# A decoder layer on one core: pieces of the first batch's scan moved ahead of the query rotations on VectorE, and the normalization in front of the feed-forward part shared out between GpSimd, ScalarE and VectorE

## The chip, the cores and the metric

The kernel runs on one core of one Trainium2 chip. The metric is the device time of one execution in microseconds (us). The program is written by hand for each engine: TensorE (PE in the profile), VectorE (DVE), ScalarE (ACT), GpSimd (POOL) and SyncE (SP) each have their own instruction stream, and they meet only at semaphores.

## The reference, cut to what matters

Four sequences ("batches") of 512 tokens with 512 features go through one decoder layer. All of it is float32.

```
x = x + attention(layernorm(x))            # 16 query heads, 2 key/value heads of 32, rotary, causal
x = x + scan(ctx, z = layernorm(x))        # selective state-space scan, 512 channels, 16 states
x = x + ffn(layernorm(x))                  # 1408 wide, 2 of 8 low-rank experts per token

layernorm(x) = (x - mean(x)) / sqrt(var(x) + 1e-5)

# scan, for each of the 16 states n (h runs over the 512 tokens):
h   = h * exp(dt * A[n]) + (dt * u) * B[n]
y  += h * C[n]                             # then y + D*u, times silu(z)
```

## The kernel before, in words

A 512x512 activation lies in SBUF as four **row tiles** of 128 tokens each, or, transposed, as four tiles of 128 features. The batches are processed one after the other, but the stages of two neighbours overlap: while the feed-forward part of batch t runs on TensorE, VectorE already works on the scan of batch t+1. The first batch has no feed-forward part in front of it, so its scan starts when its own projections start.

**The scan.** One state costs VectorE three instructions over 128x2048 elements, which the code calls pieces: `mul` (L1147, `du * B`), `run` (L1152, the scan itself) and `out` (L1157, times `C`). In front of the first `mul` stands one piece `du`. ScalarE makes `exp(dt * A[n])` for each state (L585, four instructions of 128x511, `make_decay`) and fetches the rows of B and C by DMA (L575, `load_bc`). GpSimd adds each finished state to `y_sb` by an accumulating DMA (L500, `add_states`). `state` and `decay` have two buffers, so `mul` of state n waits until state n-2 has been added, and `make_decay` of state n waits until `run` of state n-2 is done.

**The order of the work.** `plan` takes a list that says how many pieces each slot gets and lays 49 pieces (1 + 3x16) out in order. The slots are first those of the feed-forward part (none for the first batch), then 11 slots f = 0 to 10 (the down projection of the batch before; in the first batch only the projections of the attention stand there), then 32 slots s = 0 to 31, one for each pair of heads and row tile of the attention. `plan` also puts the DMA of B and C and the decay of each state into slots. For the first batch the list `PLAN_FIRST` is: one piece in each of f = 0 to 6, then `SPREAD`, which spreads the rest evenly over f = 7 to 10 and s = 4 to 30.

In slot f VectorE runs the slot's pieces and then `rotate(b, f)`: three 128x512 instructions (L1171, L1174, L1178) that turn the projection made two slots ago (f = 2 to 5 the queries, f = 6 the keys, followed by the copy of the values, L1183). TensorE makes the projections (L809) and their rotated halves (L816) in two PSUM banks; ScalarE moves each projection out of PSUM (L614, `project`). From f = 7 on the first four steps of the attention begin, the rest run in slots s. In each attention step TensorE computes scores (L848, L851), VectorE takes the row maxima (L1188) and the reciprocal of the step before (L1193), ScalarE the exponentials (L626) and moves the transposed probabilities (L638), TensorE weighs the values (L880), and VectorE divides (L1201).

**The normalization in front of the feed-forward part** (kind "ffn", `second_sum`). For each row tile VectorE adds the gated scan to x (L1263), takes mean and variance (`deviation`: L1078, L1081, L1082, L1084), and, one tile later, scales the tile before (`scaled`, L1088). GpSimd computes `(var + eps) ** -0.5` in between (`rstd`, L490). TensorE transposes each scaled tile (L967, `ffn_head`) and ScalarE moves it to `xt` (L591, `transposed_ffn`). For all but the last batch TensorE puts a projection of the next batch, two matmuls of 128x512 (L764), between the transposes of tiles 1 and 2, and ScalarE copies such projections for the convolution (L535, L536) before `transposed_ffn` and after it. When all four tiles are moved, TensorE computes the router (L971) and the wide tiles of the feed-forward part (L932).

```
for i in range(NT + 1):                                   # second_sum, before
    if i < NT:
        ...
        tt(xb[:, i, :], ps_a[:, i, :], xa[:, i, :], ALU.add).then_inc(x2_summed, 1)
        ...
        deviation("ffn", t, xb, i)
    if i >= 1:
        scaled("ffn", t, xb, xn, i - 1)
```

## Time and profile before

| | |
|---|---|
| median of 3 runs | 1403.96 us (1403.82 to 1404.07) |
| the profiled execution: its own time, its span | 1403.27 us, 1401.4 us |
| TensorE matmul busy | 1283.1 us, 92% of the span |
| VectorE busy | 1025.1 us, 73% |
| ScalarE busy | 677.3 us, 48% |
| GpSimd busy | 89.0 us, 6% |
| mean granted TensorE clock | 0.935 of full speed |
| chain that ended last, by engine | PE 61%, DVE 23%, ACT 7% |

The shares are means over stages with different limits. The 40 slices of the page give VectorE 9 or 8 tenths and TensorE 6 to 8 tenths in the slices 3 to 6 (about 70 to 245 us), with a granted clock of half speed, and from slice 8 on TensorE 8 or 9 tenths at nearly full clock. A time in a timeline is counted from the span's start. An instruction's duration reaches a little into the next one's start (pipelining), so the distance between two starts is what it takes of the engine.

### The profile page before, as it was taken

Reading aid. Unit: us, or ns where it says so; the run is one execution under the profiler, and the core shown is the slowest. Engines: PE = TensorE matmul, PEld = TensorE weight load, DVE = VectorE, ACT = ScalarE, POOL = GpSimd, SP = SyncE. Lnnn points to the kernel's source line nnn. Section 1 sums busy time; section 2 is a strip of 40 time slices with the busy share of each in tenths; the row PEclk is TensorE's granted clock in tenths of the full one; section 3 lists DMA queues with packets and bytes.
Section 4 is the critical chain, followed back from the end, with each engine's and each line's share of the span. In section 5 each row is a group of like instructions: output and inputs, shape, how many; then the busy total and the mean of one; then the engine's idle time right before and its main releaser. Section 6 shows DMA issues by size and latency. Waiting matters only on the chain.

```text
span 1401.4 us, 15839 instructions
## 1 busy us (share of the span) xinstructions
PE 1283.1 (92%) x5680; PEld 625.0 (45%) x5680; DVE 1025.1 (73%) x1238; ACT 677.3 (48%) x1465; POOL 89.0 (6%) x116
## 2 busy tenths in 40 slices
PE   5867778899999999899999999899999999799999
PEld 2334444444444465444444465444444465444443
DVE  6799997788899765888899765788899764511110
ACT  5356553465552485465552485465552385211110
POOL 0000001010000000000000000000000000100000
PEclk8855558999999999999999999999999999899999
DMA  6277663147777510147777510147777510011121
GB/s 239 57 187 147 155 138 61 46 114 192 191 188 169 158 33 1 46 115 191 191 189 168 158 32 1 46 114 191 182 187 176 145 25 9 16 38 56 57 64 52
DMA packets 53196, 158.50 MB, mean 113 GB/s; under 512 B 4992, under 2 KB 10880, under 8 KB 44672
## 3 DMA queue, kind: packets, MB, share of 16 engines
q0 software_dynamic: 9216, 67.11, 23.9%
q1 hardware_dynamic: 25520, 54.01, 11.7%
q10 hardware_dynamic: 18384, 36.37, 8.8%
q8 instruction: 46, 0.75, 0.2%
q14 instruction: 30, 0.25, 0.1%
HBM read 85.91 MB, written 4.46 MB: 64 GB/s over the span
## 4 chain that ended last, share of the span: by engine, by line
PE 61%; DVE 23%; ACT 7%; issue 4%; DMA 3%; ACTq 1%; DVEq 0%; POOL 0%
PE ps_a L932 20%; PE ps_a L946 10%; DVE state L1152 9%; PE ps_a L1023 6%; PE ps_b L957 5%; DVE state L1147 4%; PE ps_w L912 4%; PE ps_a L848 3%; ACT r L626 3%; DVE state L1157 3%; PE ps_b L865 2%; DVE neg_max L1188 2%; PE ps_a L986 2%; DMA y_sb<-state 2%; PE ps_w L880 2%
## 5 line engine op out<-in xcount | busy, mean ns | idle before, releaser
L932 PE MATMUL ps_a<-xt,w_sb 128*128 128x512 f32 x704 | 312.1, 595 | 0.0
L1152 DVE TENSOR_TENSOR_SCAN state<-decay,state 128x2048 f32<-128x2048 f32 (+1 forms) x82 | 284.4, 3477 | 2.5 <-ACT decay L585 0.6
L932 PEld LDWEIGHTS ps_a<-xt,w_sb 128*128 128x128 f32 x704 | 133.3, 191 | 170.2 <-issue 170.2
L694 ACT ACTIVATE r<-ps_a 128x512 f32<-128x512 f32 x132 | 78.5, 597 | 255.1 <-PE ps_a L946 139.0
L1334 DVE TENSOR_TENSOR r<-r,ps_a 128x512 f32<-128x512 f32 x132 | 90.0, 683 | 136.2 <-ACT r L694 136.2
L946 PE MATMUL ps_a<-r,wb_sb 128*128 128x512 f32 x352 | 165.6, 593 | 6.5 <-DVE r L1334 6.5
L585 ACT ACTIVATE decay<-dt_sb,decay_rate 128x511 f32<-128x511 f32 x256 | 163.0, 710 | 4.2 <-DVE state L1152 3.8
L626 ACT ACTIVATE r<-ps_a,neg_max 128x384 f32<-128x384 f32 (+3 forms) x224 | 121.8, 562 | 62.8 <-DVE neg_max L1188 57.2
L1157 DVE TENSOR_TENSOR state<-state,bc_sb 128x2048 f32<-128x2048 f32 (+1 forms) x73 | 147.6, 2022 | 1.5
L1147 DVE TENSOR_TENSOR state<-du_sb,bc_sb 128x2048 f32<-128x2048 f32 x64 | 146.1, 2283 | 2.9 <-DMA y_sb<-state 2.0
L865 PE MATMUL ps_b<-cst,r 128*128 128x128 f32 x640 | 109.5, 309 | 26.4 <-ACT r L626 8.8
L848 PE MATMUL ps_a<-r 32*128 32x384 f32 (+3 forms) x448 | 110.7, 575 | 22.4 <-ACT r L626 22.4
L500 POOL DMA_DIRECT2D y_sb<-state x64 | 55.9, 873 | 813.8 <-DVE state L1157 742.9
L946 PEld LDWEIGHTS ps_a<-r,wb_sb 128*128 128x128 f32 x352 | 66.2, 190 | 90.6 <-issue 87.3
L1188 DVE TENSOR_REDUCE neg_max<-ps_a 128x2 f32<-128x768 f32 (+3 forms) x112 | 95.7, 855 | 10.5 <-PE ps_a L851 8.8
L1023 PE MATMUL ps_a<-w_sb,r 128*128 128x512 f32 x224 | 101.2, 594 | 0.0
L865 PEld LDWEIGHTS ps_b<-cst,r 128*128 128x128 f32 x640 | 80.9, 159 | 38.5 <-issue 24.6
L957 PE MATMUL ps_b<-r,ad_sb 128*128 128x512 f32 x176 | 83.1, 594 | 4.9 <-DVE r L1334 4.9
L638 ACT ACTIVATE xt<-ps_b 128x256 f32<-128x256 f32 (+1 forms) x128 | 57.3, 509 | 22.2 <-PE ps_b L865 22.1
L1201 DVE TENSOR_TENSOR r<-ps_w,r 128x128 f32<-128x128 f32 x64 | 18.4, 288 | 63.5 <-ACT r L645 63.3
L1023 PEld LDWEIGHTS ps_a<-w_sb,r 128*128 128x128 f32 x224 | 41.6, 190 | 47.8 <-issue 47.8
L809 PE MATMUL ps_w<-xt,wq_sb 128*128 128x512 f32 x128 | 60.0, 614 | 2.6 <-ACT r L614 1.7
(138 smaller groups left out, 1409.3 us busy)
## 6 DMA issues: line engine op xcount, KB each, us to landing
y_sb<-state POOLq DMA_DIRECT2D x64, 1024.0 KB, 9.3
bc_sb<-bc_rows ACTq DMA_DIRECT2D x64, 512.0 KB, 6.2
w_sb<-in_w_tiles SPq DMA_DIRECT2D x44, 512.0 KB, 7.3
w_sb<-in_w_down SPq DMA_DIRECT2D x28, 256.0 KB, 3.5
wb_sb<-in_w_adapt SPq DMA_DIRECT2D x44, 128.0 KB, 2.1
xa<-in_x SPq DMA_DIRECT2D x4, 1024.0 KB, 5.2
wd_sb<-in_w_down SPq DMA_DIRECT2D x16, 256.0 KB, 7.4
out_x<-xb SPq DMA_DIRECT2D x16, 256.0 KB, 2.1
```

What stands on the lines that cost most here:

```text
L585: nc.scalar.activation(decay[:, n % 2, j, 1:L], dt_sb[:, j, 1:L], ACT.Exp, scale=decay_rate[:, j, n:n + 1]).then_inc(decay_ready, 1)
L626: nc.scalar.activation(probs[:, (2 * s + k) % 4, 0:(i + 1) * P], score_place(s, k), ACT.Exp, bias=neg_max[:, s % 2, k:k + 1], accum_out=ro ...
L848: nc.tensor.matmul(score_place(s, k), q_t[rows, m, i * P:(i + 1) * P], k_t[rows, 0:(i + 1) * P], start=True, stop=False, tile_position=(ro ...
L865: mm = nc.tensor.transpose(ps_b[:, k, kt * P:(kt + 1) * P], probs[:, (2 * s + k) % 4, kt * P:(kt + 1) * P], ident)
L932: mm = nc.tensor.matmul(ps_a[:, 2 * (f % 2) + half, :], w_sb[:, slot, at + k * P:at + (k + 1) * P], xt[:, k, :], start=(k == 0), stop=Fals ...
L946: mm = nc.tensor.matmul(ps_a[:, 2 * (f % 2) + half, :], wb_sb[:, f % 2, at:at + P], low[:, 2 * half + k - 1, :], start=False, stop=(k == 2 ...
L957: mm = nc.tensor.matmul(ps_b[:, k - 1, :], ad_sb[:, f, :], hk[:, (2 * f + k - 1) % 4, :], start=(f == 0), stop=(f == FT - 1), skip_group_c ...
L1023: mm = nc.tensor.matmul(ps_a[:, i, :], hb[:, f, i * P:(i + 1) * P], wd_ring[slot], start=(f == 0), stop=False, skip_group_check=True)
L1147: tt(state[:, n % 2, :, :], du_sb[:], row, ALU.mult).then_inc(scan_chain, 1)
L1152: done(nc.vector.tensor_tensor_scan(flat, decay[:, n % 2, tiles, :].rearrange("p j l -> p (j l)"), flat, 0.0, ALU.mult, ALU.add))
L1157: done(tt(state[:, n % 2, tiles, :], state[:, n % 2, tiles, :], row, ALU.mult))
L1188: nc.vector.tensor_reduce(neg_max[:, s % 2, :], score_pair(s), AX.X, ALU.max, negate=True)\
```

## The change

Two edits, in different stages.

**The first batch's plan.** `FIRST_DOWN` gives the slots f = 0 to 6 the counts 1, 2, 3, 1, 1, 1, 1 instead of seven ones, and the remaining 39 pieces (42 before) are spread over the same later slots. In the slots f = 1 to 10 of the first batch `make_decay` now stands ahead of `project` on ScalarE.

**The second normalization.** VectorE computes `-mean` besides `var + eps` for each tile, GpSimd computes `shift = -mean * rstd` for tiles 0 to 2 behind their `rstd`, and ScalarE computes `xn = rstd * xb + shift` for these three (`scale_normed`). VectorE scales tile 3 alone, after all four tiles' statistics. TensorE waits for tiles 0 to 2 on ScalarE's semaphore and for tile 3 on a new one.

```diff
@@ -123,8 +123,9 @@
 IN_DOWN = [1, 2, 2, 2, 2, 2, 2, 1, 1, 0, 0]
 IN_ATT = (8, 9, 11, 13, 16, 17, 19, 21)
 LAST_STEPS = 1
-SPREAD = spread_over(PIECES - (FT - EARLY), STEPS - LAST_STEPS)
-PLAN_FIRST = plan([0] * DOWN + [1] * (FT - EARLY) + SPREAD[:EARLY] + [0] * EARLY + SPREAD[EARLY:] + [0] * LAST_STEPS)
+FIRST_DOWN = [1, 2, 3] + [1] * (FT - EARLY - 3)
+SPREAD = spread_over(PIECES - sum(FIRST_DOWN), STEPS - LAST_STEPS)
+PLAN_FIRST = plan([0] * DOWN + FIRST_DOWN + SPREAD[:EARLY] + [0] * EARLY + SPREAD[EARLY:] + [0] * LAST_STEPS)
 PLAN_NEXT = plan(IN_EVALS + IN_DOWN + [int(s in IN_ATT) for s in range(STEPS)],
                  (("run", 0), ("run", NS - 1), ("out", NS - 1)))
 
@@ -257,8 +258,10 @@
         scrap_a = sb("scrap_a", [1, 1])
         stats = sb("stats", [P, NT, 6])
         mv = sb("mv", [P, NT, 2])
+        neg_mean = sb("neg_mean", [P, NT])
         var_eps = sb("var_eps", [P, NT])
         rstd = sb("rstd", [P, NT])
+        shift = sb("shift", [P, NT])
         neg_max = sb("neg_max", [P, 2, 2])
         q_bias = sb("q_bias", [P, MT])
         row_sum = sb("row_sum", [P, 2, 2])
@@ -314,6 +317,8 @@
         z_ready = sem("z_ready")
         gated_ready = sem("gated_ready")
         yt_full = sem("yt_full")
+        shift_ready = sem("shift_ready")
+        xn_ready_last = sem("xn_ready_last")
         x2_summed = sem("x2_summed")
         xt2_full = sem("xt2_full")
         xt2_moved = sem("xt2_moved")
@@ -490,6 +495,17 @@
                     nc.gpsimd.tensor_tensor(rstd[:, i:i + 1], var_eps[:, i:i + 1], cst[:, C_HALF:C_HALF + 1], ALU.pow)\
                         .then_inc(rstd_ready[kind], 1)
 
+            def shift_by_mean(t, i):
+                pool.wait_ge(rstd_ready["ffn"], t * NT + i + 1)
+                nc.gpsimd.tensor_tensor(shift[:, i:i + 1], neg_mean[:, i:i + 1], rstd[:, i:i + 1], ALU.mult)\
+                    .then_inc(shift_ready, 1)
+
+            def inverse_deviation_ffn(t):
+                for i in range(NT):
+                    inverse_deviation("ffn", t, [i])
+                    if i < NT - 1:
+                        shift_by_mean(t, i)
+
             def add_states(b, slot):
                 for n in slot["add"]:
                     pool.wait_ge(scan_chain, b * 3 * NS + 3 * n + 3)
@@ -512,14 +528,14 @@
                 add_states(0, PLAN_FIRST[DOWN + f])
             attention(0, PLAN_FIRST)
             for t in range(BATCH - 1):
-                inverse_deviation("ffn", t)
+                inverse_deviation_ffn(t)
                 for e in range(EVALS):
                     inverse_deviation("att", t + 1, NORM_AT.get(e, ()))
                     add_states(t + 1, PLAN_NEXT[e])
                 for f in range(FT):
                     add_states(t + 1, PLAN_NEXT[DOWN + f])
                 attention(t + 1, PLAN_NEXT)
-            inverse_deviation("ffn", BATCH - 1)
+            inverse_deviation_ffn(BATCH - 1)
 
 
         @block.scalar
@@ -585,8 +601,17 @@
                         nc.scalar.activation(decay[:, n % 2, j, 1:L], dt_sb[:, j, 1:L], ACT.Exp,
                                              scale=decay_rate[:, j, n:n + 1]).then_inc(decay_ready, 1)
 
+            def scale_normed(t, i):
+                act.wait_ge(shift_ready, t * (NT - 1) + i + 1)
+                nc.scalar.activation(xn[:, i, :], xb[:, i, :], ACT.Identity, bias=shift[:, i:i + 1],
+                                     scale=rstd[:, i:i + 1]).then_inc(xn_ready["ffn"], 1)
+
             def transposed_ffn(t):
+                scale_normed(t, 0)
+                scale_normed(t, 1)
                 for i in range(NT):
+                    if i == 1:
+                        scale_normed(t, 2)
                     act.wait_ge(xt2_full, t * NT + i + 1)
                     nc.scalar.activation(xt[:, :, i * P:(i + 1) * P],
                                          ps_a[:, i, :].rearrange("p (k l) -> p k l", k=KT), ACT.Copy)\
@@ -716,8 +741,8 @@
             project(0, 0)
             for f in range(1, FT):
                 load_bc(0, PLAN_FIRST[DOWN + f])
+                make_decay(0, PLAN_FIRST[DOWN + f])
                 project(0, f)
-                make_decay(0, PLAN_FIRST[DOWN + f])
                 early_steps(0, f)
             attention(0, PLAN_FIRST)
             for t in range(BATCH - 1):
@@ -962,7 +987,10 @@
                 for i in range(NT):
                     if i == 2 and t < BATCH - 1:
                         project_in(t + 1, [JT - 1])
-                    pe.wait_ge(xn_ready["ffn"], t * NT + i + 1)
+                    if i < NT - 1:
+                        pe.wait_ge(xn_ready["ffn"], t * (NT - 1) + i + 1)
+                    else:
+                        pe.wait_ge(xn_ready_last, t + 1)
                     for k in range(KT):
                         mm = nc.tensor.transpose(ps_a[:, i, k * P:(k + 1) * P], xn[:, i, k * P:(k + 1) * P], ident)
                     mm.then_inc(xt2_full, 1)
@@ -1081,12 +1109,15 @@
                 nc.vector.tensor_copy(scrap[:], vec[0:1, 0:1])
                 nc.vector.bn_aggr(mv[:, i, :], stats[:, i, :]).then_inc(norm_chain[kind], 1)
                 dve.wait_ge(norm_chain[kind], at + 2)
+                if kind == "ffn":
+                    ts(neg_mean[:, i:i + 1], mv[:, i, 0:1], -1.0, None, ALU.mult)
                 ts(var_eps[:, i:i + 1], mv[:, i, 1:2], EPS, None, ALU.add).then_inc(norm_chain[kind], 1)
 
             def scaled(kind, b, src, dst, i):
                 dve.wait_ge(rstd_ready[kind], b * NT + i + 1)
+                done = xn_ready[kind] if kind != "ffn" else xn_ready_last
                 ts(dst[:, i, :], src[:, i, :], mv[:, i, 0:1], rstd[:, i:i + 1], ALU.subtract, ALU.mult)\
-                    .then_inc(xn_ready[kind], 1)
+                    .then_inc(done, 1)
 
             def normalize(kind, b, src, dst):
                 for i in range(NT):
@@ -1263,8 +1294,7 @@
                         tt(xb[:, i, :], ps_a[:, i, :], xa[:, i, :], ALU.add).then_inc(x2_summed, 1)
                         dve.wait_ge(x2_summed, t * NT + i + 1)
                         deviation("ffn", t, xb, i)
-                    if i >= 1:
-                        scaled("ffn", t, xb, xn, i - 1)
+                scaled("ffn", t, xb, xn, NT - 1)
 
                 nc.vector.tensor_copy(scrap[:], vec[0:1, 0:1]).then_inc(x2_ready, 1)
 
```

**How the instructions move.** VectorE, first batch, from the first piece to the second rotation, before (L1147 is `mul`, L1152 `run`, L1157 `out`; L1171, L1174, L1178 are one rotation):

```order
L1147 TENSOR_TENSOR state<-du_sb,bc_sb 128x2048
L1152 SCALAR_TENSOR_TENSOR state<-decay,state 128x2048
L1171 TENSOR_TENSOR r<-r,cst 128x512
L1174 TENSOR_TENSOR r<-ps_w,cst 128x512
L1178 TENSOR_TENSOR r<-r 128x512
L1157 TENSOR_TENSOR state<-state,bc_sb 128x2048
L1171 TENSOR_TENSOR r<-r,cst 128x512
```

The same place in the changed kernel, where L1178 is `mul`, L1183 `run`, L1188 `out`, and L1202, L1205, L1209 are the rotation:

```order
L1178 TENSOR_TENSOR state<-du_sb,bc_sb 128x2048
L1183 SCALAR_TENSOR_TENSOR state<-decay,state 128x2048
L1188 TENSOR_TENSOR state<-state,bc_sb 128x2048
L1178 TENSOR_TENSOR state<-du_sb,bc_sb 128x2048
L1183 SCALAR_TENSOR_TENSOR state<-decay,state 128x2048
L1202 TENSOR_TENSOR r<-r,cst 128x512
L1205 TENSOR_TENSOR r<-ps_w,cst 128x512
L1209 TENSOR_TENSOR r<-r 128x512
L1188 TENSOR_TENSOR state<-state,bc_sb 128x2048
```

State 0's `out` and state 1's `mul` and `run` now stand ahead of the first rotation. Behind it one piece stands between two rotations, as before, up to the key rotation.

ScalarE, first batch, from the copies of the transposed input on (L598, then L623): decays are L585 and then L601, copies of a projection L614 and then L639. Before:

```order
L598 ACTIVATE xt<-ps_w 128x4x128 x4
L614 ACTIVATE r<-ps_w,q_bias 128x512
L585 ACTIVATE decay<-dt_sb,decay_rate 128x511 x4
L614 ACTIVATE r<-ps_w,q_bias 128x512 x2
L585 ACTIVATE decay<-dt_sb,decay_rate 128x511 x4
```

Now:

```order
L623 ACTIVATE xt<-ps_w 128x4x128 x4
L601 ACTIVATE decay<-dt_sb,decay_rate 128x511 x4
L639 ACTIVATE r<-ps_w,q_bias 128x512
L601 ACTIVATE decay<-dt_sb,decay_rate 128x511 x4
L639 ACTIVATE r<-ps_w,q_bias 128x512
L591 DMA bc_sb<-bc_rows 128x2x512
L601 ACTIVATE decay<-dt_sb,decay_rate 128x511 x4
L639 ACTIVATE r<-ps_w,q_bias 128x512
```

State 1's decay now stands ahead of the first copy of a projection, state 2's ahead of the second, and state 3's ahead of the third.

ScalarE at the second normalization of the first batch, before (L535 and L536 are the copies for the next batch's convolution, L591 moves a transposed tile):

```order
L535 ACTIVATE decay<-ps_w 128x512
L536 ACTIVATE decay<-ps_w,conv_half 128x512
L591 ACTIVATE xt<-ps_a 128x4x128 x4
L535 ACTIVATE decay<-ps_w 128x512
L536 ACTIVATE decay<-ps_w,conv_half 128x512
```

And now (L551, L552 and L616 are the same three, L606 is the new scaling):

```order
L551 ACTIVATE decay<-ps_w 128x512
L552 ACTIVATE decay<-ps_w,conv_half 128x512
L606 ACTIVATE r<-xb,shift,rstd 128x512 x2
L616 ACTIVATE xt<-ps_a 128x4x128
L606 ACTIVATE r<-xb,shift,rstd 128x512
L616 ACTIVATE xt<-ps_a 128x4x128 x3
L551 ACTIVATE decay<-ps_w 128x512
```

Three instructions of 128x512 come onto ScalarE here in each batch, behind the copies for the convolution and between the moves of the transposed tiles.

## Rows read from the trace of the kernel before

**Rows 1.** Windows, all engines: us, busy (count) of PE, PEld, DVE, ACT, POOL; granted clock; DMA share, GB/s

```profile
86.00:222.70 136.70, 104.59 (x694) 60.16 (x694) 134.00 (x108) 79.00 (x225) 11.27 (x13) 0.55 0.66 146
388.00:524.00 136.00, 132.38 (x747) 66.36 (x745) 113.48 (x117) 72.45 (x198) 6.98 (x9) 1.00 0.57 141
```

**Rows 2.** Timeline, VectorE, 34 to 86 us: start, duration, line, operation, idle before and releaser

```profile
34.61 4.42 DVE L1152 TENSOR_TENSOR_SCAN state<-decay,state 128x2048 f32<-128x2048 f32 x1
43.34 0.69 DVE L1171 TENSOR_TENSOR r<-r,cst 128x512 f32<-128x512 f32 x1 [4.30 <-ACT r L614]
46.91 0.69 DVE L1174 TENSOR_TENSOR r<-ps_w,cst 128x512 f32<-128x512 f32 x1 [2.88 <-PE ps_w L816]
...
61.98 0.67 DVE L1171 TENSOR_TENSOR r<-r,cst 128x512 f32<-128x512 f32 x1
...
64.08 2.29 DVE L1157 TENSOR_TENSOR state<-state,bc_sb 128x2048 f32<-128x2048 f32 x1
...
85.39 0.66 DVE L1188 TENSOR_REDUCE neg_max<-ps_b 128x2 f32<-128x512 f32 x1
```

**Rows 3.** Timeline, VectorE, two places in the attention of the first batch

```profile
91.33 2.29 DVE L1147 TENSOR_TENSOR state<-du_sb,bc_sb 128x2048 f32<-128x2048 f32 x1
93.75 4.42 DVE L1152 TENSOR_TENSOR_SCAN state<-decay,state 128x2048 f32<-128x2048 f32 x1
...
110.76 2.29 DVE L1157 TENSOR_TENSOR state<-state,bc_sb 128x2048 f32<-128x2048 f32 x1
112.97 0.42 DVE L1188 TENSOR_REDUCE neg_max<-ps_a 128x2 f32<-128x256 f32 x1
```

**Rows 4.** Groups of VectorE, 86.05 to 222.7 us: busy, mean ns, idle before

```profile
L1152 DVE TENSOR_TENSOR_SCAN state<-decay,state 128x2048 f32<-128x2048 f32 x12 | 52.9, 4410 | 0.5
L1147 DVE TENSOR_TENSOR state<-du_sb,bc_sb 128x2048 f32<-128x2048 f32 x12 | 27.3, 2276 | 0.5 <-DMA y_sb<-state 0.5
```

**Rows 5.** Timeline, PE and ScalarE at the third projection of the first batch

```profile
50.33 1.02 PE L816 MATMUL ps_w<-r,cst 128*128 128x512 f32 x2
50.53 0.69 ACT L614 ACTIVATE r<-ps_w,q_bias 128x512 f32<-128x512 f32 x1 [3.79 <-PE ps_w L809]
```

**Rows 6.** The tile y_sb, 40 to 250 us: issue to landing of the 16 accumulating DMAs

```profile
DMA to landing us min/median/max: 6.9/9.6/10.8
```

**Rows 7.** Timeline, second normalization of the second batch (its first L1263 starts at 562.53)

```profile
564.48 0.55 POOL L490 TENSOR_TENSOR rstd<-var_eps,cst 128x1 f32<-128x1 f32 x1 [4.81 <-DVE var_eps L1084]
...
566.03 0.15 DVE L1084 TENSOR_SCALAR var_eps<-mv 128x1 f32<-128x1 f32 x1
566.10 0.54 DVE L1088 TENSOR_SCALAR r<-xb,mv,rstd 128x512 f32<-128x512 f32 x1
566.26 0.78 POOL L490 TENSOR_TENSOR rstd<-var_eps,cst 128x1 f32<-128x1 f32 x1 [1.23 <-DVE var_eps L1084]
...
568.26 0.15 DVE L1084 TENSOR_SCALAR var_eps<-mv 128x1 f32<-128x1 f32 x1
...
568.92 0.66 PE L967 MATMUL ps_a<-cst,r 128*128 128x128 f32 x4 [1.58 <-DVE r L1088]
569.42 1.88 PE L764 MATMUL ps_w<-xn_att,win_sb 128*128 128x512 f32 x4
...
572.15 0.66 PE L967 MATMUL ps_a<-cst,r 128*128 128x128 f32 x4 [0.33 <-DVE r L1088]
```

**Rows 8.** Windows of PE, first L1263 to the second group of L932, batches 1, 2, 4

```profile
246.10:261.80 15.70, 12.21 (x57) 0.89 0.19 67
562.53:577.12 14.59, 10.76 (x56) 1.00 0.22 73
...
1196.22:1213.21 16.99, 11.66 (x48) 0.64 0.00 1
```

**Rows 9.** Timeline, PE in the second normalization of the first and the last batch

```profile
253.38 3.18 PE L764 MATMUL ps_w<-xn_att,win_sb 128*128 128x512 f32 x4
...
1204.85 2.10 PE L967 MATMUL ps_a<-cst,r 128*128 128x128 f32 x8 [1.12 <-DVE r L1088]
```


## The prediction

> **What bounds the kernel now.** I began with the 40 slices of the page: two regimes, a first stretch in which VectorE is full and TensorE runs at half clock, then three batches in which it is the other way round. The windows say it in numbers [rows 1]: in the attention of the first batch VectorE is busy 134.0 of 136.7 us and TensorE is granted 0.55 of its clock, while in a stretch of the same length in the next batch TensorE is busy 132.4 of 136.0 us at full clock and VectorE only 113.5. So until about 223 us the end is set by how much work VectorE has to do; after that a microsecond of VectorE is worth nothing, and only what stops TensorE counts.
>
> Next I went backwards along VectorE's timeline for idle time ahead of the full stretch [rows 2]. After the first `run` (starts at 34.61) VectorE waits 4.30 us for ScalarE's copy of the first projection, works 0.69, waits 2.88 for TensorE's rotated half, and a third wait of about half a microsecond follows. That is 7.7 us of idle time in front of a stretch of 170 us in which VectorE is never idle for long. Then I read the four places at which the feed-forward part's normalization stands: there VectorE, GpSimd, ScalarE and TensorE work one behind the other and TensorE waits [rows 7].
>
> **Edit 1: the first batch's plan.** Nothing is added; three pieces move into the idle time. I walk VectorE's queue with distances between starts. A `mul` or an `out` takes 2.2 (110.76 to 112.97), a `mul` with a `run` behind it 2.42 (91.33 to 93.75) [rows 3]; a `run` takes 4.41, less the overlap of about 0.07, 4.34 [rows 4]; behind it directly comes an `out` after 4.44; a rotation takes 2.10 (61.98 to 64.08) [rows 2].
>
> `run` 0 at 34.61, `out` 0 at 39.05, `mul` 1 at 41.25, `run` 1 at 43.67, first rotation at 48.0, `out` 1 at 50.1, second rotation 52.3, `mul` 2 54.4, third rotation 56.6, `run` 2 58.7, fourth 63.0, `out` 2 65.1, key rotation 67.4, values 69.5, `mul` 3 69.8, two maxima, `run` 3 72.65, reciprocals and `out` 3 77.1, maxima of step 2 at 79.3, `mul` 4 79.9, `run` 4 82.3, maxima of step 3 at 86.65. Before, the last stands at 85.39 [rows 2]. So VectorE gets there 1.26 us later, but with one whole state more behind it.
>
> Who waits for what was moved? The rotated half of the next projection needs the bank that the rotation before frees: the first rotation is done with it by 49.3, TensorE wants it at 50.33 [rows 5]; the later ones leave over 1 us too. ScalarE's queue now has the decay of state 3 ahead of the copy of the third projection. It waits for `run` 1 to end at 48.0 and takes 2.6, so the copy starts at 50.6 where it started at 50.53 [rows 5]: cost 0.1 us on TensorE, which waits for nothing else there. The decays of states 1 and 2 fall into ScalarE's idle time ahead of the copies. The accumulating DMA of state 0 is issued at about 41.6 instead of 51; even at 10.8 us [rows 6] it has landed when `mul` 2 asks for it at 54.4.
>
> What the later stretch saves is one state out of it: 2.20 + 4.34 + 2.20 = 8.7, and 0.4 more because `mul` is followed directly by `run` in two of the attention's slots and not in four (0.22 each). With the 1.26 that is **7.9 us**. Against it stand waits that only show once VectorE asks sooner. In step s = 5 VectorE will have only a `mul` where it had `mul` and `run`; the scores of step 6 come 0.6 to 0.7 us after it is ready for them. For other short steps I add as much again, and take off the waits of 0.5 us each that vanish. I set the net at 0.5, bounds 0 and 4. **Edit 1: 7.4 us**, 4 to 8. It all arrives at the end, since everything behind step 31 starts as much earlier.
>
> **Edit 2: the shared normalization.** For the second batch, counted from its first L1263 at 562.53: the variance of tile 1 is there at 3.50, of tile 2 at 5.73 (2.23 per tile) [rows 7]. The change takes the scaling (0.45 of VectorE's time) out of each period and adds `-mean` (0.07), so the variances come at 3.65, 5.5 and 7.4. Tile 1 then needs 0.23 to GpSimd, `rstd`, `shift`, and one ScalarE instruction of about 0.65 to 0.75, where it needed one VectorE instruction. `shift` is not in the trace; it is a 128x1 instruction like `rstd`, whose rows are 0.55 and 0.78 [rows 7]. The 0.55 stands next to VectorE's L1263, the 0.78 next to L1088. The Trainium skill (GPSIMD Engine Reference, section Key points) says that GpSimd shares its SBUF interfaces with VectorE and contends with VectorE instructions in a two-port mode or with two SBUF inputs; by that both small instructions cost 0.55, since L1088 goes away. I take 0.55 for both, as the row with the neighbour that remains, and 0.3 for GpSimd's wait on its own result (not shown; bounds 0.1 and 0.5, the latter its shortest idle time between two `rstd`).
>
> Tile 1 is transposed at 3.65 + 0.23 + 0.55 + 0.3 + 0.55 + 0.75 = 6.05 instead of 6.39 (568.92): 0.34 earlier. The projection of the next batch follows 0.5 later and takes 1.74 between starts, then tile 2 at 8.3 and, 0.6 behind it, tile 3 at 8.9 instead of 9.62 (572.15): 0.7 earlier (its own scaling would allow 8.8: 7.4 + 0.23 + 0.55 + 0.04 + 0.6). In the first and third batch this projection runs at half clock, 3.18 instead of 1.88 [rows 7, 9], and TensorE is bound from tile 1 on: only 0.34 is gained. In the last batch there is no projection, and the transposes of tiles 2 and 3 (2.10 together, the first at 1204.85, which is 8.63 behind its L1263 [rows 8, 9]) start at 5.5 + 0.23 + 0.55 + 0.3 + 0.55 + 0.75 = 7.9 and end 0.7 earlier. Sum 0.34 + 0.7 + 0.34 + 0.7 = **2.1 us**; with 0.78 for every small instruction and a wait of 0.5, tile 1 is 0.3 later than before and the sum is -0.4. With a wait of 0.1 it is 2.7. The three ScalarE instructions per batch lie in its idle time; tile 0 is held up by ScalarE's copies for the convolution and transposed some 0.7 later than now, which is hidden, as tile 1 follows no sooner.
>
> **Sum.** 7.4 + 2.1 = 9.5; the profiled execution took 1403.27, which gives 1393.8. The median of the runs is 0.7 above the profiled one, so **1394.5 us**, 0.7% faster. A difference under 0.2%, 2.8 us, I call no change.
>
> **The rivals.**
>
> *A. The freed VectorE finds the next bound at once.* The step chain (scores, maxima, exponentials, transposes) or the accumulating DMA takes back part. For it: a state takes 11.1 us in the full stretch, and a DMA up to 10.8 plus 0.3 to issue [rows 6]. Against it: VectorE waited for that DMA 0.5 us in all [rows 4], and the share of VectorE work per step stays nearly the same. If six of the eleven remaining states wait 0.7 us, 4 us are lost: 1398.5.
>
> *B. Edit 2 gives nothing.* GpSimd's second small instruction with its wait and ScalarE's queue use up what VectorE saves, so that tile 1 comes no sooner and the heads stay as long as they are. Place and price: 2.1 us, decided where GpSimd's two instructions and the wait exceed 1.7 us together. 1396.6.
>
> *C. Slower.* TensorE's clock. Of the normalizations shown, the one at full clock took 14.59 from its first L1263 to the second group of wide matmuls, the first batch's, whose clock fell in between, 15.70, the last one at a mean of 0.64 took 16.99 without a projection [rows 8]. Tile 0's transpose moves away from the projection before it, so TensorE idles longer ahead of it, about 1.9 us instead of 1.2. If the clock then stays low through the whole place in the first three batches, each costs about 16.99 + 3.0 = 20.0, which is 4.3 to 5.4 more than now, 14 us in three: 1394.5 + 2.1 + 14 = 1410.6. It turns the sign when two of the three places pay in full. Against it: the later transposes come closer together, and the same idle times led to a fall in the first batch and to none in the second. The Trainium skill (TensorE: Matmul & The Clock Gate, Part 4: PE-mode transpose) says that transposes do not count as TensorE activity the way matmuls do; by that the stretch between the two projections is idle in both kernels, and the change leaves its length nearly as it is. The rows fit it only half: the clock held in the second batch.
>
> **How the numbers follow.** The forecast has a chance of 0.68, A 0.17, B 0.10, C 0.05. The forecast's own range is 1392 to 1396.5, from the bounds of edit 1's waits, the small instructions, and a clock that may fall or not at each of four places (about 1.1 us each, the difference of 15.70 and 14.59). A and B lie above; C is left out. The range is 1391.5 to 1399.5. Faster by over 0.2%: all of the forecast and B and nearly all of A, 0.93. Slower: most of C, 0.04. Within 0.2%: 0.03.
>
> **What would show it.** In the changed profile VectorE should have no idle time of more than 0.5 us between 34.6 and 80 us; the first rotation should start at 48, the maxima of step 3 near 86.7, and the last reciprocal of the first attention, now at 222.6, near 215. From there to 1401.4 everything should stand 7.4 us earlier up to the first L1263, and tile 3's transpose 8.9 us behind it in the second batch. Waits of VectorE on ScalarE, TensorE or the DMA of over 3 us in 87 to 215 would show A; a distance of 9.6 in the normalization, B; a granted clock of half in all four normalizations, C. A first rotation that waits behind 48.0 for a projection, or an attention whose VectorE share falls under nine tenths, would make the reading of edit 1 wrong.

## The result, and the profile after

The changed kernel takes **1390.03 us** (median of 4 runs, 1388.55 to 1390.33) where the kernel before takes 1404.01 beside it: ratio 0.9895, 95% interval 0.9881 to 0.9910. The forecast was 1394.5 with a range that began at 1391.5: the direction was right, the gain, 14.0 us, half as large again as the 9.5 expected. Two more sets of runs of the same program gave 1390.60 and 1390.40 (ratios 0.9910 and 0.9907), so by the three ratios the gain is 12.6 to 14.7 us. The profiled execution has a time of its own of 1390.33 and a span of 1388.5 us; that of before had 1403.27 and 1401.4.

The page of the changed kernel: busy time of each engine, the slices of TensorE's granted clock, the chain of work that ended last by engine.

```profile
PE 1273.2 (92%) x5680; PEld 618.8 (45%) x5680; DVE 1020.9 (74%) x1242; ACT 685.5 (49%) x1477; POOL 88.5 (6%) x128
...
PEclk8857669999999999999999999999999999799999
...
PE 61%; DVE 25%; ACT 7%; issue 4%; DMA 2%; ACTq 0%; POOL 0%; DVEq 0%; POOLq 0%
```

Lines have moved: `mul`, `run`, `out` are L1178, L1183, L1188 now, the rotation L1202, L1205, L1209, the maxima L1219, the sum of the normalization L1294, its transposes L995, the variance L1114, VectorE's scaling L1119, `rstd` L495, `shift` L500, ScalarE's scaling L606, the router product L1006 (L978 before).

VectorE's timeline of the changed kernel (start, duration, line, operation, idle time before it) where [rows 2] had idle times of 4.30 and 2.88:

```profile
36.09 4.42 DVE L1183 TENSOR_TENSOR_SCAN state<-decay,state 128x2048 f32<-128x2048 f32 x1
40.55 2.29 DVE L1188 TENSOR_TENSOR state<-state,bc_sb 128x2048 f32<-128x2048 f32 x1
42.76 2.28 DVE L1178 TENSOR_TENSOR state<-du_sb,bc_sb 128x2048 f32<-128x2048 f32 x1
45.17 4.42 DVE L1183 TENSOR_TENSOR_SCAN state<-decay,state 128x2048 f32<-128x2048 f32 x1
49.52 0.67 DVE L1202 TENSOR_TENSOR r<-r,cst 128x512 f32<-128x512 f32 x1
50.10 0.68 DVE L1205 TENSOR_TENSOR r<-ps_w,cst 128x512 f32<-128x512 f32 x1
...
88.24 0.67 DVE L1219 TENSOR_REDUCE neg_max<-ps_b 128x2 f32<-128x512 f32 x1
```

No row has a bracket: nothing waits. The distances are the forecast's. From `run` 0 to the first rotation 13.43 (forecast 13.39), to the maxima of step 3 52.15 (52.04; before 50.78). Only the start has moved: `run` 0 stands at 36.09 and not at 34.61, which no edit touches; in the profiles of this study it stands anywhere from 33.2 to 37.3.

The windows of both stretches, to be read beside [rows 1], and VectorE's groups from 88.3 to 215.9 us (busy, mean ns, idle before), beside [rows 4]:

```profile
88.24:215.97 127.73, 94.81 (x691) 54.11 (x692) 125.70 (x106) 76.63 (x221) 10.29 (x12) 0.65 0.65 144
388.00:524.00 136.00, 132.40 (x858) 68.26 (x856) 109.86 (x125) 74.50 (x221) 6.94 (x8) 1.00 0.50 125
```

```profile
L1183 DVE TENSOR_TENSOR_SCAN state<-decay,state 128x2048 f32<-128x2048 f32 x12 | 52.9, 4409 | 0.4
L1188 DVE TENSOR_TENSOR state<-state,bc_sb 128x2048 f32<-128x2048 f32 x12 | 27.3, 2277 | 0.1
L1178 DVE TENSOR_TENSOR state<-du_sb,bc_sb 128x2048 f32<-128x2048 f32 x11 | 25.1, 2278 | 0.4 <-DMA y_sb<-state 0.3
...
L1232 DVE TENSOR_TENSOR r<-ps_w,r 128x128 f32<-128x128 f32 x13 | 3.6, 278 | 0.1
```

VectorE is still the bound of the first attention, 125.7 of 127.7 us. From the maxima of step 3 to the last reciprocal it took 137.2 us before; 9.5 are gone, one state (counted by their starts 11, 12 and 11 of the three large instructions instead of 12, 13 and 12; the twelfth scan of the first row is one that ends at the window's edge) and some idle time. Not all of this 9.5 is the edit's: see below, with the second edit alone.

The normalization of the second batch, all engines, to be read beside [rows 7]; its first L1294 starts at 553.44:

```profile
555.45 0.55 POOL L495 TENSOR_TENSOR rstd<-var_eps,cst 128x1 f32<-128x1 f32 x1 [4.87 <-DVE var_eps L1114]
...
556.08 0.19 POOL L500 TENSOR_TENSOR shift<-neg_mean,rstd 128x1 f32<-128x1 f32 x1
...
557.55 1.51 ACT L606 ACTIVATE r<-xb,shift,rstd 128x512 f32<-128x512 f32 x2
...
558.41 1.36 PE L995 MATMUL ps_a<-cst,r 128*128 128x128 f32 x8 [2.05 <-ACT r L606]
...
559.61 1.88 PE L789 MATMUL ps_w<-xn_att,win_sb 128*128 128x512 f32 x4
...
560.76 0.14 DVE L1114 TENSOR_SCALAR var_eps<-mv 128x1 f32<-128x1 f32 x1
...
560.98 0.55 POOL L495 TENSOR_TENSOR rstd<-var_eps,cst 128x1 f32<-128x1 f32 x1 [1.02 <-DVE var_eps L1114]
...
561.33 0.60 PE L995 MATMUL ps_a<-cst,r 128*128 128x128 f32 x4
561.56 0.55 DVE L1119 TENSOR_SCALAR r<-xb,mv,rstd 128x512 f32<-128x512 f32 x1 [0.66 <-POOL rstd L495]
...
562.16 0.66 PE L995 MATMUL ps_a<-cst,r 128*128 128x128 f32 x4 [0.23 <-DVE r L1119]
```

Tiles 0 and 1 are transposed back to back, tile 3 at 8.72 behind the first L1294 (9.62 before, forecast 8.9). `shift` takes 0.19 us and starts 0.08 behind the end of `rstd`.

TensorE's windows from the first L1294 to the second group of L957, all four batches, beside [rows 8]:

```profile
237.93:252.73 14.80, 12.01 (x56) 0.88 0.22 71
553.44:567.13 13.69, 10.68 (x55) 1.00 0.22 78
867.84:881.53 13.69, 10.67 (x55) 1.00 0.22 77
1184.06:1200.30 16.24, 12.64 (x48) 0.54 0.00 0
```

Cutting both traces at the same instructions gives the whole account (the ends are marked by starts; "place" is from the first L1263 / L1294 to the router product, and the rest ends at the first of the last four sums, L1347 / L1377):

| stretch | before | after | gain |
|---|---|---|---|
| start to `run` 0 | 34.61 | 36.09 | -1.48 |
| `run` 0 to maxima of step 3 | 50.78 | 52.15 | -1.37 |
| to the last reciprocal | 137.23 | 127.73 | 9.50 |
| to the first place (the tail) | 23.48 | 21.96 | 1.52 |
| the four places | 14.89, 13.78, 14.74, 16.18 | 13.99, 12.88, 12.88, 15.43 | 4.41 |
| between the places | 301.54, 301.57, 303.60 | 301.52, 301.52, 303.34 | 0.33 |
| rest | 183.33 | 183.33 | 0 |

That is 12.91 of the 12.94 us between the two profiled executions.

### The profile page after: what moved, and what is told of

Same layout as the page of the kernel before. It is cut to its first block, busy times and chain, and to the rows that moved or that the text cites. A ratio compares the mean times of both kernels' runs of the same rounds, so it can differ in the third digit from the quotient of the medians.

```text
span 1388.5 us, 15866 instructions
## 1 busy us (share of the span) xinstructions
PE 1273.2 (92%) x5680; PEld 618.8 (45%) x5680; DVE 1020.9 (74%) x1242; ACT 685.5 (49%) x1477; POOL 88.5 (6%) x128
## 4 chain that ended last, share of the span: by engine, by line
PE 61%; DVE 25%; ACT 7%; issue 4%; DMA 2%; ACTq 0%; POOL 0%; DVEq 0%; POOLq 0%
PE ps_a L957 20%; PE ps_a L971 10%; DVE state L1183 9%; PE ps_a L1051 6%; PE ps_b L982 5%; DVE state L1178 4%; PE ps_w L937 4%; DVE state L1188 3%; PE ps_a L873 3%; ACT r L651 3%; PE ps_b L890 2%; DVE neg_max L1219 2%; PE ps_a L1014 2%; PE ps_w L905 2%; PE ps_b L797 1%
## 5 line engine op out<-in xcount | busy, mean ns | idle before, releaser
L957 PE MATMUL ps_a<-xt,w_sb 128*128 128x512 f32 x704 | 312.3, 596 | 0.0
L1183 DVE TENSOR_TENSOR_SCAN state<-decay,state 128x2048 f32<-128x2048 f32 (+1 forms) x82 | 284.4, 3478 | 2.5 <-ACT decay L601 0.6
L957 PEld LDWEIGHTS ps_a<-xt,w_sb 128*128 128x128 f32 x704 | 133.4, 191 | 170.1 <-issue 170.1
L601 ACT ACTIVATE decay<-dt_sb,decay_rate 128x511 f32<-128x511 f32 x256 | 163.0, 710 | 7.1 <-DVE state L1183 6.7
L1188 DVE TENSOR_TENSOR state<-state,bc_sb 128x2048 f32<-128x2048 f32 (+1 forms) x73 | 147.6, 2022 | 1.5
L1178 DVE TENSOR_TENSOR state<-du_sb,bc_sb 128x2048 f32<-128x2048 f32 x64 | 146.2, 2284 | 2.5 <-DMA y_sb<-state 1.6
L890 PE MATMUL ps_b<-cst,r 128*128 128x128 f32 x640 | 104.9, 299 | 26.5 <-ACT xt L663 11.2
L873 PE MATMUL ps_a<-r 32*128 32x384 f32 (+3 forms) x448 | 107.9, 561 | 22.0 <-ACT r L651 21.9
L1219 DVE TENSOR_REDUCE neg_max<-ps_a 128x2 f32<-128x768 f32 (+3 forms) x112 | 95.8, 856 | 11.0 <-PE ps_a L876 9.1
L890 PEld LDWEIGHTS ps_b<-cst,r 128*128 128x128 f32 x640 | 77.2, 154 | 38.4 <-issue 24.8
```

What stands on the lines that cost most here:

```text
L601: nc.scalar.activation(decay[:, n % 2, j, 1:L], dt_sb[:, j, 1:L], ACT.Exp, scale=decay_rate[:, j, n:n + 1]).then_inc(decay_ready, 1)
L873: nc.tensor.matmul(score_place(s, k), q_t[rows, m, i * P:(i + 1) * P], k_t[rows, 0:(i + 1) * P], start=True, stop=False, tile_position=(ro ...
L890: mm = nc.tensor.transpose(ps_b[:, k, kt * P:(kt + 1) * P], probs[:, (2 * s + k) % 4, kt * P:(kt + 1) * P], ident)
L957: mm = nc.tensor.matmul(ps_a[:, 2 * (f % 2) + half, :], w_sb[:, slot, at + k * P:at + (k + 1) * P], xt[:, k, :], start=(k == 0), stop=Fals ...
L1178: tt(state[:, n % 2, :, :], du_sb[:], row, ALU.mult).then_inc(scan_chain, 1)
L1183: done(nc.vector.tensor_tensor_scan(flat, decay[:, n % 2, tiles, :].rearrange("p j l -> p (j l)"), flat, 0.0, ALU.mult, ALU.add))
```

## The experiments

### One edit at a time

Only the plan and ScalarE's order, on the kernel before:

```diff
-SPREAD = spread_over(PIECES - (FT - EARLY), STEPS - LAST_STEPS)
+FIRST_DOWN = [1, 2, 3] + [1] * (FT - EARLY - 3)
+SPREAD = spread_over(PIECES - sum(FIRST_DOWN), STEPS - LAST_STEPS)
...
+                make_decay(0, PLAN_FIRST[DOWN + f])
                 project(0, f)
-                make_decay(0, PLAN_FIRST[DOWN + f])
```

> The kernel before with edit 1 alone (the first batch's plan and ScalarE's order). Theory: the stretch of the first batch that VectorE bounds, from the maxima of step 3 to the last reciprocal, is 9.5 us shorter (127.7 instead of 137.2) and starts 1.4 later behind the first run, so 8.1 us come from edit 1 whatever TensorE's clock does; the tail from that reciprocal to the first L1263 (23.5 before, 22.0 in the changed kernel) goes by the clock alone and is either of the two here. Time 1394.5 to 1396. Rival: the 1.5 us of the tail belong to edit 1 and come each time, 1394.4 with a tail of 22.0 and TensorE at full clock in it. Second rival: edit 2 hides part of edit 1's gain or the other way round, then this one and edit 2 alone do not add up to 14 us.

Measured: 1393.21 us, ratio 0.9935 (0.9921 to 0.9948), below the expected range, with a tail of 22.0. One profile can't tell the theory from the first rival; the tails of all profiles are counted below, under "The tail". The second edit alone, the changed kernel with these lines put back:

> The kernel before with edit 2 alone (the shared normalization). Theory: each of the four normalizations is 0.75 to 0.9 us shorter by the engines' own times, 3.3 us in all; what the four took more than that in the changed kernel (1.86 in the third) was a clock that fell before and held after, and is there or not. Time 1400 to 1401. The first batch's stretch up to the last reciprocal is as before, 188.0 us behind the first run, and so is its tail if the clock behaves as before. Rival: the closer transposes hold TensorE's clock up, then the first and the third normalization both take 13.7 and the time is 1398.5 or less.

Measured: 1398.72 us, ratio 0.9966 (0.9954 to 0.9977). By the ratios the first edit is worth 9.1 us and the second 4.8, together 13.9 (by the medians 9.6 and 4.1): they add, and the second is worth about twice its forecast or more. This one too is faster than its theory said. In the traces the stretch to the last reciprocal is 127.75 with the plan alone and 136.75 without it. The places are 13.79, 14.89, 13.79 and 16.71 with the plan alone, 14.24, 12.88, 12.88 and 15.84 with the normalization alone; the rival wanted both the first and the third to keep the clock, and only the third did.

One expectation failed, and it bears on the first edit. From `run` 0 to the last reciprocal this run took 187.11 us, not 188.0, though its first batch is that of the kernel before; `warm_tail`, below, has the old plan too and took 187.01. Two waits of the profile before make the difference: 0.51 for the accumulating DMA, which neither of the other two has, and the first wait of [rows 2], 4.30 there against 3.88 and 3.83. From the kernel before, and from this run:

```profile
124.18 2.29 DVE L1147 TENSOR_TENSOR state<-du_sb,bc_sb 128x2048 f32<-128x2048 f32 x1 [0.51 <-DMA y_sb<-state]
```

```profile
44.35 0.69 DVE L1201 TENSOR_TENSOR r<-r,cst 128x512 f32<-128x512 f32 x1 [3.88 <-ACT r L638]
```

With `[1, 2, 3]` and the new order on ScalarE it is 179.9 in every profile. So up to the last reciprocal the first edit is worth 7.1 to 8.1 us, and the 8.13 of the table is its upper end.

The changed kernel with ScalarE's order of before (the decay behind the copy of the projection):

```diff
+                project(0, f)
                 make_decay(0, PLAN_FIRST[DOWN + f])
-                project(0, f)
```

> The changed kernel with ScalarE's order of before in slots 1 to 10 (the copy of a projection ahead of the decay). Theory: state 1's decay is made only behind the copy of the first projection (about 43.3 to 45.9 before), so run 1 waits for it from 43.7 to 46 and every later piece up to the key rotation stands some 2 us later: 2 us slower than the changed kernel, about 1392. Rival: the order does not matter, since TensorE's projections set the rotations' pace and VectorE catches up in their gaps: 1390.0.

VectorE's timeline of this run:

```profile
39.83 2.29 DVE L1178 TENSOR_TENSOR state<-du_sb,bc_sb 128x2048 f32<-128x2048 f32 x1
45.01 4.42 DVE L1183 TENSOR_TENSOR_SCAN state<-decay,state 128x2048 f32<-128x2048 f32 x1 [2.90 <-ACT decay L601]
49.36 0.67 DVE L1202 TENSOR_TENSOR r<-r,cst 128x512 f32<-128x512 f32 x1
```

`run` 1 waits 2.90 us for its decay, which stands behind the copy that waits for TensorE. From `run` 0 to the maxima of step 3 it takes 54.92 instead of 52.15. The time is 1391.82 (ratio 0.9921, 0.9908 to 0.9935), 1.8 above the changed kernel: the right sign, about the spread of such medians, so it is the trace that decides against the rival. The order of the two lines belongs to the edit.

### How many pieces

Two other lists, `[1, 2, 2]` and `[1, 3, 3]` for `[1, 2, 3]` in the first three slots.

> The changed kernel with two pieces instead of three in slot 2 (FIRST_DOWN 1, 2, 2, ...), so that state 1's run stands behind the first rotation and every later piece one place later. Theory: VectorE has the first rotation's input from 43.7 on but not its rotated half before 47, so it waits there 1 to 1.5 us; the maxima of step 3 come some 3 us earlier and one run of 4.3 us moves into the full stretch: 1 to 1.5 us slower than the changed kernel. Rival: the gain comes from the rotations being ready when VectorE comes to them, whatever the number of pieces: no difference.

> The changed kernel with three pieces in slot 1 as well (FIRST_DOWN 1, 3, 3, ...). Theory: VectorE has no idle time left between the first run and the maxima of step 3, so a further piece ahead of the rotations moves work about and hides nothing: within 0.7 us of the changed kernel, with the maxima of step 3 some 2.2 to 2.4 later and the stretch behind them as much shorter. Rival: the first rotation at 52 instead of 49.5 frees its bank behind the time at which TensorE wants it (51.8), TensorE's chain of projections moves by 1.5 us and with it the start of the attention: slower by 1 to 3 us.

Measured: 1393.59 (0.9931, 0.9919 to 0.9944) and 1392.64 (0.9918, 0.9906 to 0.9931), beside 1390.60 for the changed kernel: both slower, by 3.0 and 2.0, and by more than their theories said; the traces up to the last reciprocal show 2.3 and 0.7. From `run` 0 to the last reciprocal the traces have 188.01 us before, 182.18 with `[1, 2, 2]`, 179.88 with `[1, 2, 3]` and 180.61 with `[1, 3, 3]`. VectorE's timeline with `[1, 2, 2]`:

```profile
43.66 0.68 DVE L1202 TENSOR_TENSOR r<-r,cst 128x512 f32<-128x512 f32 x1
47.00 0.69 DVE L1205 TENSOR_TENSOR r<-ps_w,cst 128x512 f32<-128x512 f32 x1 [2.66 <-PE ps_w L841]
```

`out` 0 and `mul` 1, 4.4 us, fill the first wait of [rows 2] and leave the second, for the rotated half. With `run` 1 behind them that one is filled too. `out` 1 as well fills nothing, since nothing is idle any more. The first rotation starts 15.75 behind `run` 0, 2.3 later, and then VectorE waits 1.61 us for the scores of step 2, a wait that the changed kernel doesn't have:

```profile
85.17 0.69 DVE L1219 TENSOR_REDUCE neg_max<-ps_w 128x2 f32<-128x512 f32 x1 [1.61 <-PE ps_w L876]
```

The rival's first step is there: TensorE waits for the first rotation,

```profile
53.44 1.12 PE L841 MATMUL ps_w<-r,cst 128*128 128x512 f32 x2 [1.67 <-DVE r L1205]
```

and the maxima of step 0 now stand behind `run` 3 on VectorE and start 4.5 us later behind `run` 0 (41.96 for 37.47); which of the two makes the scores late is not separated. The maxima of step 3 stand 1.6 later, and the attention gives back only 0.9 of it. The idle time was 7.7 us, and the three pieces that the change moves ahead of the first rotation take 2.2 + 2.4 + 4.4 = 9.0; the 1.3 too many are what the second stretch of the table lost (1.37).

### GpSimd's part and ScalarE's share

A spare multiply ahead of each `shift`:

```diff
+                nc.gpsimd.tensor_tensor(spare[:, i:i + 1], neg_mean[:, i:i + 1], rstd[:, i:i + 1], ALU.mult)
                 nc.gpsimd.tensor_tensor(shift[:, i:i + 1], neg_mean[:, i:i + 1], rstd[:, i:i + 1], ALU.mult)\
```

> The changed kernel with a second small GpSimd multiply ahead of each shift, so that ScalarE's scaling of tiles 0, 1 and 2 starts 0.2 us later. Theory (VectorE's four periods and its own scaling of tile 3 bound the feed-forward part's normalization; GpSimd and ScalarE have slack): from the first L1294 to the router product 12.88 us in the batches at full clock, as in the changed kernel, and the time within 0.5 us of it (0.990 to 0.992 of the kernel before). Rival, the forecast's pricing (tile 1 by way of the shift sets the place): 13.1 at full clock, 0.8 us over four batches.

Measured: 1389.37, ratio 0.9904 (0.9889 to 0.9920), places 14.13, 12.88, 12.89 and 15.96. The theory holds: `shift` has slack. The places that keep the clock moved by no more than a hundredth.

Tiles 2 and 3 scaled by VectorE, after the last sum, and only 0 and 1 by ScalarE:

```diff
-                    if i < NT - 1:
+                    if i < NT - 2:
                         shift_by_mean(t, i)
...
+                scaled("ffn", t, xb, xn, NT - 2)
                 scaled("ffn", t, xb, xn, NT - 1)
```

> The changed kernel with tiles 0 and 1 scaled by ScalarE and tiles 2 and 3 by VectorE at the end. Theory (what the edit is worth is that no scaling stands between two of VectorE's sums): tile 2's scaling fits into the 0.66 us in which VectorE waits for the last inverse deviation, so tile 3's scaling starts when it did (8.1 us behind the first L1294), and the distance stays at 12.9 to 13.0 at full clock; time within 0.5 us of the changed kernel. Rival (each tile that ScalarE takes is worth its share): 0.3 to 0.5 us later in each batch, 1.5 in all.

Measured: 1391.61, ratio 0.9921 (0.9905 to 0.9937). The place at full clock takes 13.11, 0.23 more than the changed kernel's 12.88: between theory and rival. The timeline of VectorE and GpSimd at its end says why:

```profile
559.54 0.54 DVE L1117 TENSOR_SCALAR r<-xb,mv,rstd 128x512 f32<-128x512 f32 x1
559.71 0.78 POOL L495 TENSOR_TENSOR rstd<-var_eps,cst 128x1 f32<-128x1 f32 x1 [1.29 <-DVE var_eps L1112]
...
560.52 0.55 DVE L1117 TENSOR_SCALAR r<-xb,mv,rstd 128x512 f32<-128x512 f32 x1 [0.44 <-POOL rstd L495]
```

The scaling of tile 2 does fit into VectorE's wait, as the theory had it. But beside it `rstd` of tile 3 takes 0.78 instead of 0.55, and that is the path. So the third tile on ScalarE is worth a quarter of a microsecond, by what it takes away from beside GpSimd. The Trainium skill (GPSIMD Engine Reference, section 1, Specifications) says that GpSimd shares its SBUF interfaces with VectorE and contends with its instructions in a two-port mode or with two SBUF inputs. 0.55 where no scaling of VectorE runs beside it and 0.78 beside L1117 agree; that L1117 runs in such a mode is not shown by any run.

### The clock ahead of the attention's end

The kernel before, with the transposes of steps 20 to 29 of the first attention made twice:

```diff
+                    for again in range(1 + (first_batch(b) and 20 <= s < STEPS - 2)):
+                        for kt in range(i + 1):
```

> The kernel before, where TensorE makes the transposes of the probabilities twice in the steps 20 to 29 of the first batch (the same result written again, some 1 us of TensorE per step in time that it idles). Theory: the tail of the first batch, 23.5 us from the last reciprocal to the first L1263 at a clock that is at half in part of it, is 22.0 us when TensorE comes in at full clock, so 1.5 us faster than before, 1402.5, with the stretch that VectorE bounds unchanged at 137.2. Rival: TensorE's extra work gets in the way of the steps and VectorE waits for it: the stretch grows by more than 1.5 us and the time is 1404 or more. Second rival: the tail does not hang on the clock and stays at 23.5 at full clock.

Measured: 1403.97, ratio 1.0003 (0.9994 to 1.0012). The stretch behind the last reciprocal stays at 23.55. Its windows, TensorE first, the granted clock third from the end:

```profile
214.00:220.00 6.00, 5.55 (x43) 2.98 (x41) 5.97 (x2) 2.10 (x6) 0.00 (x0) 1.00 0.33 67
220.00:224.00 4.00, 0.01 (x1) 0.04 (x1) 2.39 (x5) 2.25 (x7) 0.88 (x1) 1.00 0.49 98
224.00:228.00 4.00, 4.00 (x41) 2.94 (x42) 1.67 (x7) 1.81 (x4) 0.56 (x1) 0.57 0.82 168
```

The clock was full up to 224 and fell all the same. TensorE reached the place earlier and so idled longer there, 4.45 us ahead of the last transposes instead of 2.39, since what ends this idle time is ScalarE, not TensorE. Work ahead of an idle stretch did not protect what came behind it. The run did not bring about what it was to test, a tail at full clock, so it decides neither for the theory nor for the second rival.

### Products into the idle time of the last batch

In the last batch there is no projection to put between the transposes, and the place takes 15 to 16 us there. First, three unused projections ahead of it (`keep_busy`: products of `win_sb` and `ctx_sb` into the two free banks):

```diff
+            keep_busy(BATCH - 1, 2)
             transpose_gated(BATCH - 1)
+            keep_busy(BATCH - 1, 1)
             ffn_head(BATCH - 1)
```

> The changed kernel with three unused projections (two matmuls of 128x512 each) on TensorE in the last batch, where the other batches have theirs: two in front of the transposes of the gated tiles, one behind them. Theory: the last normalization takes 15.4 to 15.9 us to the router's last product because the clock falls in TensorE's idle time ahead of it, and 12.9 in the others; kept busy it takes 12.2 to 12.9 (no projection stands between its transposes) and the transposes of the gated tiles are 0.5 to 1 us quicker: 3 to 3.5 us faster than the changed kernel. Rival: the extra matmuls delay the transposes they stand in front of (3.6 us in an idle time of 4.9, 1.9 in one of 1.3), and what the clock gives is paid back: 0 to 1 us.

Measured: 1390.02, ratio 0.9907 (0.9894 to 0.9919), place 15.96. The clock held until about 1188 us and fell between the transposes; the half-speed stretch moved behind the place, where the rest took 185.29 instead of 183.33. The transposes of the gated tiles took 1.97 instead of 3.67. No gain over 1390.60: the rival's time, though what ate the gain was the clock's later fall.

Then also between the tiles, in single products: 8 ahead of the gated transposes, 6 ahead of tile 0, 2 ahead of tile 2; and the same without the first 8.

```diff
                         project_in(t + 1, [JT - 1])
+                    elif i == 2:
+                        keep_busy(t, 2)
...
+            keep_busy(BATCH - 1, 8)
             transpose_gated(BATCH - 1)
+            keep_busy(BATCH - 1, 6)
```

> The changed kernel with 16 unused matmuls of 512 columns in the last batch: 8 ahead of the transposes of the gated rows, 6 ahead of tile 0 of the normalization and 2 ahead of tile 2, where TensorE otherwise idles. Theory (in the last batch the normalization takes 15.0 to 16.0 us instead of 12.9 because TensorE has no projection to do there and its clock falls): the granted clock stays at 1.00 through the place, the distance from the first L1294 to the router product falls to 12.9 to 13.5, the time by about 2 us, 1388. Rival (the unused products cost what they save, or the clock falls all the same, as it did at 1188 us with products ahead of the place alone): 15 to 16 us, 1390 to 1391.

> As the run before, without the 8 products ahead of the transposes of the gated rows. If the idle time of 4.9 us ahead of those transposes is what the clock falls in, the clock is at half from 1184 us on and the distance is 15 to 16 us; if the products within the place suffice to hold or bring back the clock, it is under 14 us.

Measured: 1390.74 (0.9914, 0.9898 to 0.9929) with 16, clock 1.00 throughout and the place at 13.37, but the 8 products lasted 7.10 us where only 4.0 were idle, and the stretch ahead of the place grew to 304.47. Without the 8: 1389.54 (0.9901, 0.9885 to 0.9918); the clock fell in the idle 4.87 us, the six products, partly at half clock, took 6.46 us and pushed tile 0 back, place 15.72. Products did hold the clock, and products behind its fall did bring it back, and in both runs they cost what they gave. So the sizes were wrong, and the last pair fits them to the idle time (4, 4 and 2 products):

> The changed kernel with 10 unused products in the last batch, sized to the idle time that the run with 16 left visible: one product is 0.89 us at full clock; ahead of the transposes of the gated rows TensorE idles 4.87 us, of which 0.88 is a wait for a bank, so 4 (3.6 us) instead of 8; ahead of tile 0 it idles 3.9, so 4 instead of 6; 2 ahead of tile 2 as before. Theory (with 16 the clock held and the place took 13.37 us instead of 15.4, but the surplus products pushed the gated transposes back by as much as was won): clock 1.00 through the place, 12.9 to 13.0 us from the first L1294 to the router product, and from the last batch's start to its end (gap, place and rest together) 498 to 499.5 us where the changed kernel has 500.5 to 502.1; 2 us off the median. Rival (idle pieces of under a microsecond between the products let the clock fall again): 15 to 16 us in the place, no gain.

> The changed kernel again, beside the run with 10 unused products, and a third profile of it: one of the first three normalizations at 13.9 to 14.2 us and two at 12.88, the last at 15.0 to 16.0, the time from the last rotation maximum to the last reciprocal 127.7, the stretch behind it 22.0 or 23.5.

Measured: **1386.51** (1386.47 to 1388.83), ratio 0.9885 (0.9868 to 0.9901), beside 1390.40 (1389.18 to 1391.50), ratio 0.9907 (0.9892 to 0.9922), for the changed kernel. TensorE's timeline with the products (L991; one product is two matmuls in it), the first sum of the place at 1182.74:

```profile
1177.98 3.67 PE L991 MATMUL ps_w<-xn_att,win_sb 128*128 128x512 f32 x8 [0.88 <-DVE xa L1290]
1181.97 1.97 PE L945 MATMUL ps_a<-cst,r 128*128 128x128 f32 x16 [0.32 <-DVE r L1299]
1183.78 3.60 PE L991 MATMUL ps_w<-xn_att,win_sb 128*128 128x512 f32 x8
1187.21 0.60 PE L1005 MATMUL ps_a<-cst,r 128*128 128x128 f32 x4
1188.31 0.66 PE L1005 MATMUL ps_a<-cst,r 128*128 128x128 f32 x4 [0.50 <-ACT r L606]
```

and of the changed kernel beside it:

```profile
1182.16 3.68 PE L945 MATMUL ps_a<-cst,r 128*128 128x128 f32 x16 [4.87 <-DVE r L1287]
1187.11 1.12 PE L995 MATMUL ps_a<-cst,r 128*128 128x128 f32 x4 [1.28 <-ACT r L606]
1188.95 1.12 PE L995 MATMUL ps_a<-cst,r 128*128 128x128 f32 x4 [0.72 <-ACT r L606]
```

The transposes of a tile take 0.60 to 0.66 instead of 1.12, and the place 12.88, to a hundredth what it takes in the batches with a projection, instead of 14.96. TensorE has more to do here and is through 2.1 us sooner, so it is the clock that makes the last batch's place longer than the others. From the third router product to the first of the last four sums it is 499.56 us instead of 500.36 to 502.10 in three profiles of the changed kernel. That is 0.8 to 2.5; the medians are 3.9 apart, and how much of the rest is chance stays open, as 4 runs each are few. No run of the one reaches a run of the other beside it (1388.83 and 1389.18), but the changed kernel's first set has a run of 1388.55. This version has the lowest median of the study.

The changed kernel again, beside the doses and the first products:

> The changed kernel itself, as the yardstick for the other kernels of this group. Theory: the two edits add (9.6 and 4.1 us alone), so 13 to 14 us faster than before, and in the trace the stretch from the maxima of step 3 to the last reciprocal is 127.7 again; the first run, the tail and the first normalization vary with the granted clock by up to 1.5, 1.5 and 1.1 us. Rival: the first result was a lucky draw of the clock, then it is 11.5 us faster or less.

Measured: 1390.60, ratio 0.9910 (0.9898 to 0.9923), 12.6 us faster and so a little under the theory's 13 to 14, and above the rival's 11.5. With `after_third` there are three profiles of it. In the changed kernel everything set by VectorE repeats to 0.02 us (52.14 to 52.15, 127.72 to 127.73). What TensorE's clock sets does not: the stretch behind the last reciprocal is 21.96, 23.55, 23.56, and the places 13.99, 12.88, 12.88; 12.88, 14.17, 12.89; 12.88, 14.18, 12.89.

## Where the prediction was wrong, and where it was right

The result lies below the forecast's range, because the gain was larger than forecast. Two steps failed. The sum had no term for the tail behind the first attention ("everything behind step 31 starts as much earlier"), which gave 1.5 us; and edit 2 was put at 2.1 us, with 2.7 as its most, and gave 4.4. The directions and the places were right.

**What bounds: right.** VectorE in the first attention, TensorE behind it. What was won ahead of 216 us arrived whole at the end: the stretches between the places changed by 0.33 us in all and the rest by nothing.

**Edit 1, the queue: right.** Each distance up to the maxima of step 3 came out within 0.12 us, no wait is left between `run` 0 and 80 us, and neither the decay nor the accumulating DMA was late there.

**Edit 1, the net of the waits: at most 0.7 us off, and not shown to be off.** "Against it stand waits that only show once VectorE asks sooner", a loss of 0.5. Against the profile before, the stretch shrank by 9.5 and the walk grew by 1.37 (forecast 1.26), net 8.13 for 7.4. There the idle time in the groups fell from 2.6 to 2.1: the wait for the divide's operand went from 0.6 to 0.1, the one for the DMA from 0.5 to 0.3, and the one for the scores rose from 0.3 to 0.5. But in the two other profiles with the old plan, the gain is 7.2 and 7.1 (187.11 and 187.01 to 179.9), and their stretch has no wait for the DMA at all. So 7.4 lies among the three, and up to 0.9 us of the 8.13 is the luck of the profile before. Rival A fell: of the 4 us that it wanted lost there are 0.5 for the scores and 0.3 for the DMA.

**The tail: no term was there.** The stretch behind the last reciprocal gave 1.52 us. Of all profiles it has two lengths, 22.0 in 9 of 13 profiles with the new plan, 23.5 in the other four and in all three with the old one. It is decided at one spot: TensorE idles 1.5 to 2.6 us for ScalarE ahead of its last transposes (4.45 in `warm_tail`), and eight of them take 1.1 us where the clock holds and 1.3 to 1.8 where it falls, with everything up to the next projection slower behind them. Before, in the changed kernel, and in its third profile (`after_third`):

```profile
224.98 1.69 PE L865 MATMUL ps_b<-cst,r 128*128 128x128 f32 x8 [2.39 <-ACT xt L638]
```

```profile
218.32 1.12 PE L890 MATMUL ps_b<-cst,r 128*128 128x128 f32 x8 [1.79 <-ACT xt L663]
219.37 0.42 PE L900 MATMUL ps_w<-cst,row_inv 128*32 128x128 f32 x8
```

```profile
216.90 1.32 PE L890 MATMUL ps_b<-cst,r 128*128 128x128 f32 x8 [1.90 <-ACT xt L663]
218.16 0.66 PE L900 MATMUL ps_w<-cst,row_inv 128*32 128x128 f32 x8
```

With `[1, 2, 2]` the clock held over 2.63 us, so the length alone does not decide. That the new plan shifts the odds is suggested by the counts and not shown; the old plan has only three profiles.

**Edit 2: mis-sized, 4.4 us for 2.1, beyond its own bound of 2.7.** Three terms. (1) `shift` was priced as `rstd`, 0.55, and a wait of GpSimd on itself as 0.3; measured 0.19 and 0.08. That "it is a 128x1 instruction like `rstd`" led to the wrong neighbour: a multiply is not a power. With them, tile 1 is transposed 5.7 behind the first sum and not 6.05, tile 3 is bound by VectorE's own path alone, and at full clock the place is 0.90 shorter (13.78 to 12.88), not 0.7. (2) "TensorE is bound from tile 1 on: only 0.34 is gained" was too little for the first batch, which also gave 0.90 (14.89 to 13.99): the projection behind tile 1 started 0.61 sooner, and less of it ran at half clock, so that it took 0.28 less. (3) The third place kept its clock, 14.74 to 12.88, which is 0.96 on top. The last batch gave 0.75 for 0.7. Of the first three places, two, two and one were slow in the three profiles with the old normalization, and one, never none, in 11 of 13 with the new one, two in the other two. So some of this third term is probably the edit's and some the draw; the runs don't separate them. Rival B fell: GpSimd's two instructions and the wait take 0.82 us together (0.55 + 0.08 + 0.19) where it wanted over 1.7, and edit 2 alone is worth 4.1 by the medians.

**The clock as a range: right in kind, used too timidly.** A swing of 1.1 us per place was named, and the measured falls are 0.9 to 1.4 there, 1.6 in the tail and 2.1 to 3.1 in the last batch. The range ended at 1391.5; the bounds of edit 1 (8), edit 2 (2.7) and two draws (2.2) off 1403.27 + 0.7 give 1391.1, and with the tail as one more place (1.5) 1389.6, which holds the result. Rival C had the mechanism right and the sign wrong: the idle time ahead of tile 0 did grow, from 1.17 to 2.06 us, yet the clock was lost no more often in the counts above.

**The median.** 0.7 was added for the distance of the profiled execution to the median; in the changed kernel it is -0.3. With 8.13 - 7.4, 1.52, 4.41 - 2.1, 0.33 and -1.48 (the start) the miss of 3.4 in the trace is complete, and this 1.0 makes it 4.4; the rest of the 4.5 is rounding. Luck stands on both sides of this sum: the start cost 1.48, which no edit touches, and the tail, the third place and the waits of the profile before gave up to 1.5, 1.0 and 0.9. That the medians of three sets of runs lie between 1390.0 and 1390.6 says that the gain as a whole, 12.6 us or more, is no draw.

## What to carry to other kernels

Idle time in front of a full engine is worth filling piece by piece until the last wait is gone and no further, and the producer's queue must be reordered with it. Price a small instruction by its operation, not by its size, and ask what runs beside it. Take more than one profile of the kernel before, too: a wait that is in one and not in the next is no cost of the plan. Where TensorE waits in short gaps in front of much work, read the granted clock there: products whose results nobody uses, sized to the gap in microseconds, gave back 2.1 us in one place here (10 products), and 16 of them gave nothing.

## What the runs showed of the hardware

- On GpSimd a multiply of 128x1 takes 0.19 us, a power of 128x1 0.55, and 0.78 when it runs beside a 128x512 scaling on VectorE (`norm_two`); in the changed kernel a dependent one starts 0.08 us behind the first.
- ScalarE scales and shifts a 128x512 tile from SBUF in 0.81 us, two in 1.51; VectorE needs 0.55.
- The clock fell behind an idle stretch of 4.45 us although TensorE had been busy at full clock until then (`warm_tail`). In the last batch 4.87 us of idle time stand ahead of the gated transposes, and in every profile that left them open the sixteen transposes took 3.4 to 3.7 us; in the three that filled them the clock held and they took 1.9 to 2.0. Where idle time is shorter, the same program with the same distances lost the clock in the first place in one profile and in the second in two. The Trainium skill (TensorE: Matmul & The Clock Gate, Part 4: PE-mode transpose) says that transposes do not count as activity like matmuls; by that the products, not the transposes, hold the clock in the last batch. The run with products ahead of the place alone, whose clock fell among the transposes, agrees, but idle time lay there too, so no run here separates the two.
